# Softplus of a selective-scan layer as max(x, 0) + log(1 + exp(-|x|)), with the absolute value on ScalarE

## What is computed

```python
xi, z = split(x @ W_in.T)                      # 512 channels each
u  = silu(causal_conv4(xi) + conv_b)
dbl = u @ W_xproj.T                            # 16 ranks, 16 B, 16 C
dt = softplus(dbl[..., :16] @ W_dt.T + b_dt)   # the part that changes
dA = exp(dt[:, :, None] * A)                   # 16 states for each channel
h  = h * dA + (dt * u)[:, :, None] * B;  y = sum(h * C)
x  = layernorm(x + (y + u * D_skip) * silu(z) @ W_out.T)
x  = layernorm(x + (silu(x @ wg.T) * (x @ wu.T)) @ wd.T)
```

## Time and profile before

| | us |
|---|---|
| median of 3 runs (lowest, highest) | 1962.93 (1960.35, 1966.26) |
| the profiled execution's own time | 1964.99 |
| its span, first to last instruction | 1962.9 |
| busy in the span: TensorE, VectorE, ScalarE, GpSimd | 1777.8, 1705.2, 1665.8, 1496.4 |
| mean granted TensorE clock | 0.982 of full speed |

### The profile page before, as it was taken

How to read it: one execution, slowest core, us unless ns; L and a number is a source line. 1 busy time by engine, 2 the same in 40 slices (tenths; PEclk the granted TensorE clock), 3 DMA queues, 4 the chain that set the end, 5 groups by cost and what they waited for, 6 DMA issues and landing times.

```text
span 1962.9 us, 40142 instructions
## 1 busy us (share of the span) xinstructions
PE 1777.8 (91%) x15616; PEld 1205.0 (61%) x15616; DVE 1705.2 (87%) x1924; ACT 1665.8 (85%) x2899; POOL 1496.4 (76%) x848
## 2 busy tenths in 40 slices
PE   4769999999999998999989999998999989898987
PEld 2446665666656575666666656576666666566664
DVE  4799898989989899898989999899998989989852
ACT  5798889898898979889898888989888898988941
POOL 2787977778797877977777797877878777798830
PEclk8899999999999999999999999999999999999998
DMA  6030121211112120131212012121111212021000
GB/s 193 3 109 1 3 108 14 98 24 51 69 4 98 25 97 24 4 117 4 97 25 95 25 3 97 25 97 24 45 76 3 97 25 97 24 64 46 1 23 11
DMA packets 171036, 100.54 MB, mean 51 GB/s; under 512 B 139344, under 2 KB 157008, under 8 KB 162656
## 3 DMA queue, kind: packets, MB, share of 16 engines
q1 hardware_dynamic: 170848, 97.98, 17.3%
HBM read 88.52 MB, written 9.44 MB: 50 GB/s over the span
## 4 chain that ended last, share of the span: by engine, by line
PE 38%; DVE 24%; ACT 18%; issue 10%; POOL 5%; DMA 5%; ACTq 0%; DVEq 0%; SPq 0%; POOLq 0%
PE ring L865 14%; DVE h L702 12%; PE tp L844 10%; PE ring L953 7%; ACT decay L526 5%; ACT hT L533 5%; DVE acc L723 5%; POOL drive L407 4%; PE yb L858 4%; ACT res L592 3%; DMA res<-in_x 3%; DVE dt L731 2%; DMA out<-res 2%; ACT xi L544 1%; ACT dt L580 1%
## 5 line engine op out<-in xcount | busy, mean ns | idle before, releaser
L407 POOL TENSOR_TENSOR drive<-dtu,b_all 128x1024 f32<-128x1024 f32 x512 | 1218.9, 2407 | 58.7 <-DVE h L702 55.8
L526 ACT ACTIVATE decay<-dt,a_neg 128x512 f32<-128x512 f32 x1024 | 700.9, 706 | 78.6 <-DVE h L702 72.9
L844 PE MATMUL tp<-ident,h 128*128 128x128 f32 x4096 | 589.5, 280 | 127.1 <-ACT hT L533 101.5
L844 PEld LDWEIGHTS tp<-ident,h 128*128 128x128 f32 x4096 | 459.5, 142 | 379.2 <-ACT hT L533 159.8
L702 DVE TENSOR_TENSOR_SCAN h<-decay,h,drive 128x512 f32<-128x512 f32 x512 | 627.2, 1270 | 46.9 <-ACT decay L526 39.0
L533 ACT ACTIVATE hT<-tp 128x512 f32<-128x512 f32 x1024 | 584.9, 604 | 91.8 <-PE tp L844 90.8
L702 DVE TENSOR_TENSOR_SCAN h<-decay,drive 128x512 f32<-128x512 f32 x512 | 597.3, 1210 | 60.5 <-ACT decay L526 46.7
L858 PE MATMUL yb<-hT,diag_c 128*32 128x128 f32 x8192 | 278.5, 279 | 0.0
L865 PE MATMUL ring<-xt,w_in 128*128 128x512 f32 x512 | 247.3, 607 | 11.4 <-DMA w_in<-in_W_inT 6.4
L858 PEld LDWEIGHTS yb<-hT,diag_c 128*32 128x32 f32 x8192 | 212.8, 111 | 46.1 <-issue 40.5
L865 PE MATMUL ring<-xt,w_g 128*128 128x512 f32 x384 | 184.1, 603 | 2.2 <-DVE xi L757 1.4
(11 more groups left out here) (67 smaller groups left out, 1527.9 us busy)
## 6 DMA issues: line engine op xcount, KB each, us to landing
b_all<-bc_scratch SPq DMA_DIRECT2D x64, 1024.0 KB, 9.1
xt<-in_xT SPq DMA_DIRECT2D x16, 512.0 KB, 4.8
res<-in_x SPq DMA_DIRECT2D x16, 512.0 KB, 4.0
out<-res SPq DMA_DIRECT2D x16, 512.0 KB, 2.9
c_col<-bc_scratch SPq DMA_DIRECT2D x256, 2.0 KB, 2.5
w_in<-in_W_inT SPq DMA_DIRECT2D x2, 512.0 KB, 5.1
bc_scratch<-dbl SPq DMA_DIRECT2D x16, 64.0 KB, 1.6
w_g<-in_w_gT SPq DMA_DIRECT2D x1, 768.0 KB, 7.5
```

The lines of the kernel that those rows point to most:

```text
L407: tt(drive[:, j % 4, :, :], src, b_all[:, n:n + 2, :], ALU.mult).then_inc(g_dr, 1)
L526: act(decay[decay_slot(k.parity, i)][:, :], dt[:, cb, :], ACT.Exp, scale=a_neg[:, cb, n:n + 1]).then_inc(a_da, 1)
L844: last = nc.tensor.transpose(tp[g % 2][:, b * P:(b + 1) * P], h[:, h_slot(k.parity, q), t0:t0 + TS, :].rearrange("p t s -> p (t s)"), iden ...
```

## The change

For each half, VectorE no longer clamps. ScalarE takes |x| of `acc` into `dt`, then exp(-|x|), then ln(1 + that). VectorE's last step computes max(x, 0) + dt in one scalar_tensor_tensor in place of the maximum. The two waits of the clamp move into the function on ScalarE, and a wait of Exp for the Abs takes the place of its wait for the clamp. The places in the order are kept; the entries of the clamp go.

```diff
-    (0, -1): [("clamp", 1)], (0, 3): [("max", 1)], ...
+    (0, 3): [("max", 1)], ...
-    ... (14, 1): [("clamp", 0)], (14, 3): [("skip", 2)],
+    ... (14, 3): [("skip", 2)],
             def softplus_log(k, half):
                 two = dt[:, 2 * half:2 * half + 2, :]
-                wait(eng, v_mn, k.count(2, half + 1))
-                act(two, two, ACT.Exp).then_inc(a_e, 1)
+                wait(eng, a_xb, k.count(4, 2 * half + 2))
+                wait(eng, a_da, k.count(STEPS, -STEPS + 32 * (half + 1)))
+                act(two, acc[:, 2 * half:2 * half + 2, :], ACT.Abs).then_inc(a_abs, 1)
+                eng.wait_ge(a_abs, k.count(2, half + 1))
+                act(two, two, ACT.Exp, scale=-1.0).then_inc(a_e, 1)
                 eng.wait_ge(a_e, k.count(2, half + 1))
                 act(two, two, ACT.Ln, bias=1.0).then_inc(a_ln, 1)
-            def clamp(k, half):
-                two = slice(2 * half, 2 * half + 2)
-                wait(eng, a_xb, k.count(4, 2 * half + 2))
-                wait(eng, a_da, k.count(STEPS, -STEPS + 32 * (half + 1)))
-                ts(dt[:, two, :], acc[:, two, :], 40.0, None, ALU.min).then_inc(v_mn, 1)
-            def softplus_max(k, half):
+            def softplus_sum(k, half):
                 two = slice(2 * half, 2 * half + 2)
                 wait(eng, a_ln, k.count(2, half + 1))
-                tt(dt[:, two, :], acc[:, two, :], dt[:, two, :], ALU.max).then_inc(v_dt, 1)
+                stt(dt[:, two, :], acc[:, two, :], 0.0, dt[:, two, :], ALU.max, ALU.add).then_inc(v_dt, 1)
...
-            clamp(k0, 0)
-            softplus_max(k0, 0)
+            softplus_sum(k0, 0)
```

More of the change, by code:

```diff
@@ L83 @@
 DVE_SIDE = {
-    (0, -1): [("clamp", 1)], (0, 3): [("max", 1)], (2, 1): [("conv", 0, 0), ("conv", 0, 1), ("skip", 3)],
+    (0, 3): [("max", 1)], (2, 1): [("conv", 0, 0), ("conv", 0, 1), ("skip", 3)],
     (4, 2): [("r1", 0), ("conv", 1, 0)],
@@ L89 @@
     (11, 1): [("skip", 1)], (11, 3): [("gs", 4)], (12, 0): [("hid", 3)], (13, 0): [("hid", 4)],
-    (13, 1): [("gs", 5)], (13, 3): [("hid", 5)], (14, 1): [("clamp", 0)], (14, 3): [("skip", 2)],
+    (13, 1): [("gs", 5)], (13, 3): [("hid", 5)], (14, 3): [("skip", 2)],
     (15, 1): [("r2", 0), ("max", 0)], (15, 3): [("r2", 1)],
@@ L275, in mamba_ffn @@
         a_da = sem("a_da"); a_ev = sem("a_ev"); a_xi = sem("a_xi"); a_u = sem("a_u"); a_z = sem("a_z")
-        a_sz = sem("a_sz"); a_xb = sem("a_xb"); a_dbl = sem("a_dbl"); a_e = sem("a_e"); a_ln = sem("a_ln")
+        a_sz = sem("a_sz"); a_xb = sem("a_xb"); a_dbl = sem("a_dbl"); a_abs = sem("a_abs"); a_e = sem("a_e"); a_ln = sem("a_ln")
         a_y = sem("a_y"); a_x1T = sem("a_x1T"); a_th = sem("a_th"); a_x1 = sem("a_x1"); a_o = sem("a_o"); a_set = sem("a_set")
-        v_h = sem("v_h"); v_y = sem("v_y"); v_conv = sem("v_conv"); v_mn = sem("v_mn"); v_dt = sem("v_dt")
+        v_h = sem("v_h"); v_y = sem("v_y"); v_conv = sem("v_conv"); v_dt = sem("v_dt")
         v_r1 = sem("v_r1"); v_s1 = sem("v_s1"); v_gs = sem("v_gs")
@@ L775, in side @@
                 for what, i, *part in DVE_SIDE.get((q, j), []):
[L776 to L780, removed]
                     if what == "max":
                         if i == 1:
-                            softplus_max(k, 1)
+                            softplus_sum(k, 1)
                         elif head:
-                            softplus_max(k + 1, 0)
+                            softplus_sum(k + 1, 0)
                     if what == "conv" and head:
```

## The result

| | before | after |
|---|---|---|
| median of 5 runs (lowest, highest), us | 1964.39 (1960.35, 1966.26) | 1975.92 (1973.7, 1977.14) |
| span of the profiled execution, us | 1962.9 | 1974.2 |

The changed kernel is slower: ratio 1.0060, 95% interval 1.0045 to 1.0074. That is 11.5 us between the medians and 11.3 us between the spans. The forecast was 1977 us.

A forecast was written before the change was run, and what follows sets the result against it. ScalarE's order was taken to bound the chunk boundaries, VectorE following its decays. Half 0's +14.65 and half 1's -0.15 gave +14.5 us on the median 1962.93, so 1977.4 us (chance 0.76); range 1963 to 1985.

The forecast's parts named there:

- A: Chunk boundary like the one at 480 to 515 us, 7 of 15; half 0 there regains 0.15 us each.
- B: Chunk boundary like the one at 598 to 635 us, 7 of 15, the last included; 0.05 us slack at each.
- The Abs of half 0: Ahead of hT 55 on ScalarE: nothing hides it, so 15 boundaries by 1.09 us, +16.35 us.
- Half 1 is neutral: ScalarE's log of half 1: Abs fills the wait for the clamp, 1.00 us where it was 1.18 or 0.92.
- No further table load: Rival, much slower: Abs outside the loaded table adds loads of 1.28 us, 79 us in all, 2057 us; chance 0.03.
- the wait of decay 61: ScalarE, half 0: the clamp delays scan 58, which decay 61 awaits; removing it regains 7 x 0.15 = 1.05 us.
- the order of ScalarE sets the pace, and VectorE follows the decays: Claimed bound at chunk boundaries: ScalarE full for 9.97 and 9.98 of 10 us, VectorE with 0.8 to 1.0 us of room.
- half 0 (+14.65): Sum for half 0 over all boundaries: Abs +16.35, less 1.05, 0.35 and 0.3 us regained.
- half 1 (-0.15): Sum for half 1: filled waits -0.8, first boundary's Abs +1.09, last boundary's diagonals on GpSimd -0.44 us.
- my bound of 1.58: VectorE's new last step, upper bound 1.58 us against 1.33 us for a plain tensor_tensor; cost foretold 0.
- VectorE's head start: Some 2.5 us at a boundary from the removed clamp, taken as lost; rival that it is kept: 1943 us, chance 0.09.
- half 0's Abs would be absorbed: Rival, same within 0.3%: ScalarE's 3.67 us idle time at B absorbs the delay, 1963 us; chance 0.12.

The follow-up runs named there:

- Experiment 1: The change made for one half only, each against the kernel before: half 0 alone ratio 0.9968 (median 1960.3 us), half 1 alone 0.9966 (1958.2 us).
- two moves: Kernel before with VectorE's clamp of half 1 earlier: 1.0006; with GpSimd's std 1 moved behind drives 5 and 6: 0.9975; with both: 0.9908.

## Why the prediction was right, and where it was not

**Right.** The sign and the size: +14.5 us foretold, 11.5 measured. On the path over ScalarE each term came out to some hundredths at A and B. The Abs of half 0 delays `down` 1 by 1.09 us at each boundary (table load to residual step, 10.48 before, 11.56 after). Half 1 is neutral on that path: from the residual step to Ln 5.50 and 5.24 us before, 5.30 after, so -0.20 and +0.06, where -0.18 and +0.08 were foretold. Abs takes 1.06 us, and the next instruction starts 1.09 us after it. No further table load appears; the Trainium skill, "ScalarE: Activation LUTs", section "Table sets: the hidden batching unit", had said so, and the 15 loads at L624 agree. ScalarE stays full behind the log (10.00 of 10 us). At A the wait of decay 61 is gone: the three decays ahead of the table load take 1.91 us, where they took 2.06. That the total came out within 3 us is in part luck, since the misses in the table below go both ways.

**Wrong: "the order of ScalarE sets the pace, and VectorE follows the decays."** In the kernel before, GpSimd's path reached skip 3 after ScalarE's, by 0.37 us at A, 0.19 at B and 1.1 at the first boundary. The sum has no term for it. ScalarE's path grew by 0.87 us at A and 1.13 at B, and only what went beyond that lead was paid: from the table load to skip 3 the boundary grew by 0.50 and 0.95 us. Over the 14 boundaries this is 4.9 us that my sum should have taken off. Here is the whole sum beside what the two traces show, in us:

| stretch | foretold | measured |
|---|---|---|
| start to the first table load | -0.3 | -0.9 |
| first boundary, table load to skip 3 | +2.2 | +1.4 |
| 7 boundaries A, the same | +6.4 | +3.5 |
| 6 boundaries B, the same | +6.7 | +5.7 |
| from skip 3 to the next table load, 14 stretches | -1.1 | +0.8 |
| last table load to the end | +0.6 | +0.7 |
| sum | +14.5 | +11.2 |

The 14 stretches between move by up to 1.1 us each, either way, and in other kernels by up to 2.1. What moves them is left open. In all traces of this document the shift of skip 3 at the 13 boundaries between the first and the last gives the change of the span to within 5 us.

**Wrong: the split into half 0 (+14.65) and half 1 (-0.15).** The sum holds only for both together. Experiment 1 shows what the split left out: the clamp's 2.69 us in half 1 was not a price of its own but an overlap with GpSimd's drives, and a delay ahead of it shrinks it. Half 0 alone moves `down` 1 by 1.09 us, and ScalarE's wait of 1.18 or 0.92 us goes by itself. Half 1, changed on top of that, then pays for its Abs in full: ScalarE's path goes from 31.39 to 32.45 us. So the same loss could as well be booked on half 1.

**The cost that I had bounded.** The new last step on VectorE takes 1.19 us in half 0, like the maximum, but 3.15 to 3.35 us in half 1, over my bound of 1.58, since it starts in the middle of GpSimd's drives. It costs nothing, as foretold: VectorE still waits 0.50 us for a decay behind it, at the row of 517.51.

**The rivals.** VectorE's head start brought nothing, as ScalarE's decays held it. That half 0's Abs would be absorbed was true in a way that I had not seen: alone it is absorbed, by a shrinking clamp, not by idle time. Together it is not, but GpSimd's lead still absorbs the first 0.37 or 0.19 us of it.

## What to carry to other kernels

An instruction that another engine stretches hides a wait that no list shows: the convolution's 2.67 us look like work, and the chain of waits walked past them to TensorE. Compare the duration of a row with the shortest of its kind before calling an engine the bound. When two paths end within a few tenths of a microsecond, price a change on both, and test two moves together before saying that either is worthless: here two moves worth nothing and 0.25% alone gave 0.92% as a pair. And before adding work to an engine, look where it stands idle for another reason; the same Abs cost 1.0% or nothing by its place.

## What the runs showed of the hardware

VectorE instructions with two SBUF sources, and the clamp with one, run long when they start while a GpSimd tensor_tensor is running, and end after it: the clamp of 128x1024 takes 0.67 us with GpSimd idle and up to 2.71 us beside a drive; the last step of the softplus 1.19 and up to 3.35 us. The end comes at a fixed distance behind the end of the GpSimd instruction: in the traces before and after 0.54 to 0.56 us for all 16 clamps and 20 steps of the convolution that began beside one, 1.08 to 1.09 us for all 30 last steps of the softplus. GpSimd pays too: its diagonals take 1.05 us alone and 1.49 to 1.52 us beside a clamp. Scans, whose decay comes from PSUM, were not stretched (1.19 to 1.34 us, beside such instructions and without them). The Trainium skill, "GPSIMD Engine Reference", section "1. Specifications", names VectorE instructions with two SBUF inputs, and those in a 2-port performance mode, as contending with GpSimd for SBUF. For the first kind the traces agree; that the clamp runs in such a mode is not shown, though it is stretched in the same way. The price in these traces is about the rest of the GpSimd instruction that is running.
